# Self-attention: amplitude chain and logits ahead of two heads' sums, router's product two slots sooner, four heads' scores at once in the short tiles

## The chip, the cores and the metric

One core of a Trainium2 chip. The time is that of one execution on the device, in microseconds (us). The core has five engines with a queue each: PE (TensorE: matrix products and transposes), DVE (VectorE), ACT (ScalarE), POOL (GpSimd) and SP (SyncE, which here only issues DMAs). Every queue runs in its own order, and the queues meet at semaphores.

## The reference, cut to what matters

```python
x = x + cross_attention(layernorm(x), ctx)       # 2 x 512 rows, 2 x 8192 keys, 16 heads of 32
x = x + self_attention(layernorm(x))             # 2 x 512 rows, causal, 16 heads of 32
x = x + experts(layernorm(x))                    # 16 experts, top 2, capacity

# self attention, for a row x of 512:
q_amp, k_amp = softplus(x @ Wq_amp.T), softplus(x @ Wk_amp.T)       # split into 16 heads
q_phi, k_phi = pi * tanh(x @ Wq_phi.T), pi * tanh(x @ Wk_phi.T)
q_amp, k_amp = each / sqrt(mean(each ** 2 over the head) + eps)
scores = (q_amp cos q_phi . k_amp cos k_phi + q_amp sin q_phi . k_amp sin k_phi) / sqrt(32) * exp(scale)
out    = softmax(causal(scores)) @ (x @ Wv.T);  x = x + out @ Wo.T

# experts: logits = layernorm(x) @ w_router, softmax, top 2, rows of each expert counted in order
```

## The kernel before

The first 1550 us or so are the cross-attention. The change lies in the stage behind it, the self-attention, which runs from about 1550 us to about 1840 us of the profile; the experts follow to the end.

The 1024 rows are 8 row tiles t of 128 (four for each of two batches). Tile t attends to the tiles of its batch up to itself, so it has 1, 2, 3 or 4 blocks of 128 keys: `qb = t % 4`, `nk = 128 * qb + 128`. The 16 heads are taken in 8 pairs, so there are 64 steps p, with tile `a = p // 8` and pair `p % 8`. Two steps make a group of four heads, n = p // 2.

`self_order` writes out one list of pieces by hand, and each engine walks the list and emits its own part of each piece. Hence the place of a piece in the list is its place in the queue of the engine that does it. I call the 8 steps of a tile a block, numbered 0 to 7. A block has 16 slots k, two for each step, emitted by `slot(a, k)`. While block a attends, `ahead(a + 1, k)` prepares tile t = a + 1, and `follow` finishes tiles a - 1 and a - 2.

What `ahead` emits for tile t in block t - 1:
- slots 0 to 3: `p23` (PE, the product for the phases in four parts, banks 2 and 3), and on ACT `abs`, `exp`, `ln` (softplus of the amplitudes in banks 0 and 1, L1617 to L1625), `relu` (L1612) in slot 1, which frees banks 0 and 1
- slot 3 `amp` (DVE L1941: softplus finished), slot 4 `square` (DVE L1955) and `turn` (PE L1274: transposes the next tile), slot 5 `phase` and `mean` (DVE L1959, L1962)
- `phase` is a chain on ACT: a table load (L1509), Tanh (L1640), Sin (L1644), a wait for `tabs` (DVE L1973, the absolute value of the phase), Sin with a bias for the cosine (L1647), and a table load back (L1509)
- slot 6 `tabs`, and `p4` (PE, the product for the values, in two parts, bank 1); slot 7 the second part of `p4`, `copy` (ACT) and `low` (DVE L1951) of the next tile, and `mroot` (ACT L1514, L1516: the reciprocal root of the mean)
- slot 8 `vcopy` (ACT) and `norm` (DVE L1758 to L1968: a Newton step on the root, then the amplitudes are scaled); slots 9 and 10 `polar` 0 and 1 (DVE L1979: amplitude times cosine and sine); from slot 10 `qkT` (PE L1302: transposes of queries and keys), `qkC` (their copies), and the next tile's `p01` (PE)

What a step p does besides: `scoreT` (PE L1332: scores of a pair into banks 4 and 5; it waits until the step before has been read), `expT` (ACT L1671: exp of the pair into `pT`), and for each group n `cut` (DVE L2021, L2027: the causal mask on the last block of keys, then the blocks are added), `valueT` (PE L1347, L1351: the heads' sums over the keys; it waits for `cut`), and `normT` (DVE L2033, L2037: divides; it waits for `valueT`). `valueT` of group 4a stands behind slot 5 of block a.

Behind tile a - 1 follow `wo0` and `wo1` (PE L1362, slots 6 and 7), `x3` and the statistics; behind tile a - 2 come `router` (PE L1417, slot 4, bank 1) and `logit` (DVE L2058, L2061, slot 5), which frees bank 1 for `p4`. In block 1 a `colsum` (PE L1411) and `negsum` (DVE L2065) stand in their place, in block 6 also `cum` (PE L1425) and `place` (DVE L2114).

The queue of block a = 2 on PE, between its second and its sixth group of scores, is therefore: scoreT 17, p23, p23, scoreT 18, turn, router, valueT 8, scoreT 19, p4, wo0, p4, wo1, scoreT 20, valueT 9, scoreT 21, qkT.

A second list (`kept`) serves another numerical path, which is not taken with these inputs; `slot` and `ahead` are shared with it.

## Time and profile before

| | us |
|---|---|
| median of 3 runs | 1967.76 (1967.36 to 1967.77) |
| the profiled execution | 1968.28 |
| its span | 1966.5 |
| span busy: PE / DVE / ACT | 1898.0 / 1712.3 / 1470.9 |

The profile is one execution, recorded by the hardware. The rows further down come from four of its views: busy time in given stretches, with the clock that TensorE was granted (1.00 is full speed); the list of who waited for whom; the instructions in order of time; and instructions grouped by line. A name such as L1332 is a line of the kernel. An engine's row in the order of time ends with its idle time and the instruction that ended it, where there was any.

### The profile page before, as it was taken

To read this page: it belongs to the slowest core of one execution; us is meant where nothing else is said; L and a number is where in the kernel's file an instruction comes from. 1 tells how busy PE (TensorE), PEld (TensorE's weight loads), DVE (VectorE), ACT (ScalarE), POOL (GpSimd) and SP (SyncE) were. 2 spreads that over 40 slices of the span, in tenths; PEclk is the share of its full clock that TensorE was granted. 3 is DMA by queue.
4 is the path that set the end of the run, shared out by engine and by line. 5 is a ranking of instruction groups with operands and counts; after the bars stand their busy time and mean duration, and the time that the engine had idled before them with its cause. 6 is when DMAs were issued, how large, how long until landed. Compare 5 with 4: busy or idle time off the path is not lost.

```text
span 1966.5 us, 31028 instructions
## 1 busy us (share of the span) xinstructions
PE 1898.0 (97%) x11704; PEld 744.4 (38%) x11704; DVE 1712.3 (87%) x1530; ACT 1470.9 (75%) x1676; POOL 46.9 (2%) x57
## 2 busy tenths in 40 slices
PE   8999999999999999999999999999998989999895
PEld 4333333333333333333333333333332345556431
DVE  5799999999999999979999999999997578788655
ACT  2588888888888888778888888888887455555221
POOL 2000000000000000000000000000000000001103
PEclk9999999999999999999999999999999989999998
DMA  8333333333333333322332233333323000004785
GB/s 256 114 89 106 96 91 97 97 102 97 102 90 88 91 97 97 108 65 74 95 90 81 81 87 89 93 88 90 91 71 113 23 1 1 1 1 176 256 303 166
DMA packets 113674, 194.57 MB, mean 99 GB/s; under 512 B 10353, under 2 KB 64625, under 8 KB 113521
## 3 DMA queue, kind: packets, MB, share of 16 engines
q1 hardware_dynamic: 110528, 183.33, 31.8%
q0 software_dynamic: 2560, 8.39, 1.3%
q8 instruction: 98, 1.61, 0.3%
q10 hardware_dynamic: 432, 0.79, 0.1%
q14 instruction: 56, 0.45, 0.1%
HBM read 109.63 MB, written 50.33 MB: 81 GB/s over the span
## 4 chain that ended last, share of the span: by engine, by line
PE 87%; DVE 6%; issue 2%; ACT 2%; DMA 1%; POOL 1%; POOLq 0%; SPq 0%; DVEq 0%; ACTq 0%
PE ps L1204 24%; PE ps L1449 23%; PE ps L1103 12%; PE ps L1100 12%; PE ps L1293 2%; PE ps L1231 2%; PE ps L1288 2%; PE ps L1140 2%; PE ps L1256 1%; PE ps L1188 1%; PE ps L1332 1%; PE ps L1302 1%; DVE dacc L1860 1%; PE ps L1362 1%; ACT pt L1712 1%
## 5 line engine op out<-in xcount | busy, mean ns | idle before, releaser
L1712 ACT ACTIVATE pt<-ps,bias 128x1024 f32<-128x1024 f32 x1024 | 1108.7, 1114 | 212.3 <-PE ps L1449 211.3
L1860 DVE TENSOR_TENSOR dacc<-dacc,pt 128x2048 f32<-128x2048 f32 x496 | 1134.9, 2288 | 59.6 <-ACT pt L1712 35.9
L1449 PE MATMUL ps<-qst,kst 128*128 128x512 f16 x2048 | 611.1, 381 | 7.9 <-ACT pt L1712 7.9
L1204 PE MATMUL ps<-pt,vt 128*32 128x512 f32 x4096 | 493.4, 598 | 0.0
L1449 PEld LDWEIGHTS ps<-qst,kst 128*128 128x128 f16 x2048 | 178.1, 98 | 413.7 <-ACT pt L1712 123.3
L1103 PE MATMUL ps<-wsm 128*128 128x512 f16 x1152 | 310.8, 380 | 0.0
L1100 PE MATMUL ps<-wsm 128*128 128x512 f16 x1116 | 301.4, 379 | 0.0
L1204 PEld LDWEIGHTS ps<-pt,vt 128*32 128x32 f32 x4096 | 106.7, 109 | 262.6 <-issue 240.6
L1103 PEld LDWEIGHTS ps<-wsm 128*128 128x128 f16 x1152 | 112.8, 98 | 138.1 <-issue 3.3
L1100 PEld LDWEIGHTS ps<-wsm 128*128 128x128 f16 x1116 | 109.0, 98 | 133.1 <-issue 2.2
L1803 DVE SCALAR_TENSOR_TENSOR wsm<-ps,wsm 128x512 f16<-128x512 f32 x126 | 86.4, 686 | 26.2 <-ACT wsm L1533 26.2
L1671 ACT ACTIVATE pT<-ps 128x256 f32<-128x256 f32 (+3 forms) x64 | 44.5, 701 | 55.5 <-PE ps L1332 55.2
L1871 DVE TENSOR_TENSOR oacc<-ps,oacc 128x512 f32<-128x512 f32 x120 | 82.1, 684 | 2.3 <-PE ps L1209 2.3
L1537 ACT ACTIVATE vt<-ps 128x512 f32<-128x512 f32 x128 | 76.3, 596 | 3.8 <-PE ps L1103 3.8
L1533 ACT ACTIVATE wsm<-ps 128x512 f16<-128x512 f32 x126 | 74.4, 591 | 0.0
L2182 DVE SCALAR_TENSOR_TENSOR wsm<-wsm 128x512 f16<-128x512 f32 x90 | 61.5, 683 | 0.0
L1050 POOL DMA_INDIRECT xbuf<-xn,diu x13 | 14.3, 1097 | 1782.8 <-DVE diu L2131 1779.5
L1720 ACT ACTIVATE wsm<-wsm 128x512 f16<-128x512 f32 x90 | 55.8, 620 | 0.0
L1332 PE MATMUL ps<-QT,KT 64*128 64x128 f32 x640 | 53.1, 295 | 2.6 <-ACT pT L1671 2.2
L1293 PE MATMUL ps<-wsm,xT 128*128 128x512 f16 x216 | 50.8, 380 | 4.8 <-DVE negs L2065 2.3
L1332 PEld LDWEIGHTS ps<-QT,KT 64*128 64x128 f32 x640 | 41.5, 190 | 23.7 <-issue 23.7
L2033 DVE RECIPROCAL pr<-ps 128x128 f32<-128x128 f32 x32 | 30.5, 952 | 19.2 <-PE ps L1351 16.2
(228 smaller groups left out, 1201.2 us busy)
## 6 DMA issues: line engine op xcount, KB each, us to landing
kst<-kscr SPq DMA_DIRECT2D x132, 256.0 KB, 3.4
kscr<-wsm SPq DMA_DIRECT2D x126, 256.0 KB, 3.5
kst<-kst SPq DMA_DIRECT2D x124, 256.0 KB, 3.4
wsm<-in_ctx SPq DMA_DIRECT2D x31, 768.0 KB, 5.1
wx<-in_gate SPq DMA_DIRECT2D x10, 512.0 KB, 8.8
wx<-in_fc SPq DMA_DIRECT2D x10, 512.0 KB, 9.4
wx<-in_proj SPq DMA_DIRECT2D x10, 512.0 KB, 9.2
qst<-qscr SPq DMA_DIRECT2D x32, 128.0 KB, 3.0
```

The costliest lines, as they stand in the source:

```text
L1100: p = e.matmul(ps[:, at, :], wk[:, wi, c, u * 128:u * 128 + 128], chl[:, j, ci_, c, :], start=n == 0, stop=n == 8)
L1103: p = e.matmul(ps[:, at, :], chl[:, j, ci_, c, u * 128 - 512:u * 128 - 384], wv[:, wi, c, :], start=n == 0, stop=n == 8)
L1204: p = e.matmul(ps[32 * h:32 * h + 32, 4 + n % 2, :], vt[:, kb % 2, ch, c:c + 32], pt[:, (2 * i + h // 2) % 6, h % 2, :], start=ch == 0, st ...
L1293: p = e.matmul(ps[:, b0 + n, :], xhl[:, t % 2, xi, c * 128:c * 128 + 128], whl[w0 + n][:, wi, c, :], start=m == 0, stop=m == 11)
L1332: m = e.matmul(ps[:, bk + h, 128 * k:128 * k + 128], KT[64 * h:64 * h + 64, hp, c:c + 128], QT[64 * h:64 * h + 64, t % 3, hp, :], start=Tr ...
L1449: p = e.matmul(ps[:, 2 * half + h2, :], kst[:, kb % 2, h, ch * 128:ch * 128 + 128], qst[:, h, :], start=True, stop=True)
L1533: e.activation(halves(kb, u)[:, 0], ps[:, at, :], ACT.Copy, scale=KS / (WS * CS)).then_inc(S["khi"], 1)
L1537: e.activation(vt[:, j, u - 4, :], ps[:, at, :], ACT.Copy, scale=1.0 / (WS * CS)).then_inc(S["vev"], 1)
L1712: e.activation(pt[:, (2 * i + half) % 6], ps[:, 2 * half:2 * half + 2, :], ACT.Exp, bias=bias[:, 4 * kb + ch:4 * kb + ch + 1], scale=SCORE ...
L1803: e.scalar_tensor_tensor(out=hl[:, 1], in0=ps[:, at, :], scalar=KS / (WS * CS), in1=hl[:, 0], op0=ALU.mult, op1=ALU.subtract).then_inc(S[" ...
L1860: e.tensor_tensor(own_heads, own_heads, probs, ALU.add).then_inc(S["add"], 1)
L1871: e.tensor_tensor(oacc[:, g, :], ps[:, 4 + n % 2, :], oacc[:, g, :], ALU.add).then_inc(S["oac"], 1)
```

## The change

In `ahead` the amplitude pieces go up: `amp`, `square` and `mean` follow `ln` in slot 2, `mroot` stands ahead of `phase` in slot 5, and `norm` behind `tabs` in slot 6. On DVE they thereby stand ahead of `normT` of group 4a - 1 and `cut` of group 4a, and on ACT the root is taken ahead of the phase's table load. In `slot` the router's product and `colsum` go from slot 4 to slot 2 ahead of `p23`, and `logit` and `negsum` from slot 5 to slot 2, behind `mean`. `valueT` of group 4a goes from behind slot 5 to behind slot 6, hence behind the first part of `p4` and `wo0`. Block 7 keeps its order. `pairs_of(p)` is 2 for even and 0 for odd steps in tiles with one or two blocks of keys (blocks 0, 1, 4, 5): there `scoreT` and `expT` take two pairs at once, the second pair in the upper half of the same two banks, so that 16 of the 64 `scoreT` and `expT` fall away.

```diff
--- before.py
+++ after.py
@@ -459,32 +459,32 @@
             out.append((("abs", "exp", "ln")[slot], t))
         if slot == (1 if t else 3) and t < 7:
             out.append(("xn", t + 1))
-        if slot == 3:
+        if slot == (2 if t else 3):
             out.append(("amp", t))
             if t < HALVES:
                 empty((0, 1), "amp", t + 1)
-        elif slot == 4:
             out.append(("square", t))
+            out.append(("mean", t))
+        if slot == 4:
             if t < 7:
                 turn(t + 1)
         elif slot == 5:
+            out.append(("mroot", t))
             out.append(("phase", t))
             empty((2, 3), "phi", t + 1)
-            out.append(("mean", t))
         elif slot == 6:
             out.append(("tabs", t))
+            out.append(("norm", t))
             p4(t, 0)
         elif slot == 7:
             if t < 7:
                 out.append(("copy", t + 1))
                 if t + 1 >= HALVES:
                     out.append(("low", t + 1))
-            out.append(("mroot", t))
             p4(t, 1)
             empty((1,), "sv", t + 1)
         elif slot == 8:
             out.append(("vcopy", t))
-            out.append(("norm", t))
         elif slot == 9:
             out.append(("polar", t, 0))
         elif slot == 10:
@@ -536,29 +536,33 @@
 
     def slot(a, k):
 
+        if a == 6 and k == 2:
+            out.append(("cum", 0, 1, fill((1,))))
+        if a == 1 and k == 2:
+            out.append(("colsum", 0, fill((1,))))
+            empty((1,), "lg", 1)
+        if 2 <= a < 7 and k == 2:
+            follow(a - 2, "router")
         if a < 7:
             ahead(a + 1, k)
+        if a == 1 and k == 2:
+            out.append(("negsum", 0))
+        if 2 <= a < 7 and k == 2:
+            follow(a - 2, "logit")
+        if a == 6 and k == 2:
+            out.append(("place", 0, 1))
+            empty((1,), "cumr", 1)
         if 1 <= a < 8:
             for step in (carry if a < 7 else late).get(k, ()):
                 follow(a - 1, step)
-        if a == 6 and k == 4:
-            out.append(("cum", 0, 1, fill((1,))))
-        if a == 1 and k == 4:
-            out.append(("colsum", 0, fill((1,))))
-            empty((1,), "lg", 1)
-        if a == 1 and k == 5:
-            out.append(("negsum", 0))
         if (a, k) in halving:
             out.append(halving[a, k])
-        if 2 <= a < 8 and k == (4 if a < 7 else 1):
+        if a == 7 and k == 1:
             follow(a - 2, "router")
-        if 2 <= a < 8 and k == (5 if a < 7 else 2):
+        if a == 7 and k == 2:
             follow(a - 2, "logit")
         if a == 5 and k in (6, 8, 9, 11, 13):
             out.append((("rank", "odds", "first", "second", "shares")[(6, 8, 9, 11, 13).index(k)], 0))
-        if a == 6 and k == 5:
-            out.append(("place", 0, 1))
-            empty((1,), "cumr", 1)
         if a == 6 and k == 7:
             out.append(("rows", 0))
 
@@ -623,11 +627,13 @@
     else:
         for p in range(64):
             a, k = p // 8, 2 * (p % 8)
-            if p <= 56:
+            if p <= 56 and pairs_of(p):
                 out.append(("scoreT", p, ()))
             if 56 <= p < 63:
                 out.append(("scoreT", p + 1, fill((0, 1)) if p == 56 else ()))
             slot(a, k)
+            if p % 8 == 3 and a < 7:
+                out.append(("valueT", p // 2 - 1))
             if p == 63:
                 out.append(("rank", 1))
                 out.append(("first", 1))
@@ -635,13 +641,14 @@
                 out.append(("moments", 4 + k // 4))
             if p == 8:
                 out.append(("stats", 1))
-            out.append(("expT", p))
+            if pairs_of(p):
+                out.append(("expT", p))
             if p % 2:
                 if p > 2:
                     out.append(("normT", p // 2 - 1))
                 out.append(("cut", p // 2))
             slot(a, k + 1)
-            if p % 2 == 0 and p:
+            if p % 2 == 0 and p and (p % 8 != 2 or a == 7):
                 out.append(("valueT", p // 2 - 1))
         ahead_of_last()
         out.append(("woT", 7, 0, 3, (("prob", 63),)))
@@ -675,6 +682,11 @@
 
 def score_bank(p):
     return 0 if p >= 56 and p % 2 else 4
+
+
+def pairs_of(p):
+
+    return (2 if p % 2 == 0 else 0) if p // 8 % 4 < 2 else 1
 
 
 def turn_bank(j):
@@ -1326,12 +1338,13 @@
                     e.wait_ge(S["KT"], 2 * t + hp // 4 + 1)
                     if x is not None:
                         e.wait_ge(S["prob"], x + 1)
-                    for k in range(qb + 1):
-                        for h in range(2):
-                            c = 128 * ((4 * b + k) % 5)
-                            m = e.matmul(ps[:, bk + h, 128 * k:128 * k + 128], KT[64 * h:64 * h + 64, hp, c:c + 128],
-                                         QT[64 * h:64 * h + 64, t % 3, hp, :], start=True, stop=True)
-                    m.then_inc(S["score"], 1)
+                    for j in range(pairs_of(p)):
+                        for k in range(qb + 1):
+                            for h in range(2):
+                                c, o = 128 * ((4 * b + k) % 5), 256 * j + 128 * k
+                                m = e.matmul(ps[:, bk + h, o:o + 128], KT[64 * h:64 * h + 64, hp + j, c:c + 128],
+                                             QT[64 * h:64 * h + 64, t % 3, hp + j, :], start=True, stop=True)
+                    m.then_inc(S["score"], pairs_of(p))
                 elif what == "valueT":
                     n, t, g, u = t, t // 4, t % 4, t % 2
                     qb, b = t % 4, t // 4
@@ -1665,11 +1678,16 @@
                                      scale=-1.0, accum_out=rsum[:, s:s + 1]).then_inc(S["prob"], 1)
                 elif what == "expT":
                     p, n, bk, nk = t, t // 2, score_bank(t), 128 * (t // 8 % 4) + 128
-                    e.wait_ge(S["score"], p + 1)
+                    e.wait_ge(S["score"], p + pairs_of(p))
                     if n > 1:
                         e.wait_ge(S["value"], n - 1)
-                    e.activation(pT[:, n % 2, 2 * (p % 2):2 * (p % 2) + 2, 0:nk], ps[:, bk:bk + 2, 0:nk], ACT.Exp,
-                                 scale=-1.0).then_inc(S["prob"], 1)
+                    if pairs_of(p) == 2:
+                        e.activation(pT[:, n % 2, :, 0:nk].rearrange("p (j h) n -> p j h n", j=2),
+                                     ps[:, bk:bk + 2, :].rearrange("p h (j n) -> p j h n", j=2)[:, :, :, 0:nk], ACT.Exp,
+                                     scale=-1.0).then_inc(S["prob"], 2)
+                    else:
+                        e.activation(pT[:, n % 2, 2 * (p % 2):2 * (p % 2) + 2, 0:nk], ps[:, bk:bk + 2, 0:nk], ACT.Exp,
+                                     scale=-1.0).then_inc(S["prob"], 1)
                 elif what == "pT" and t % 2:
                     n, nk = t // 4, 128 * (t // 16 % 4) + 128
                     e.wait_ge(S["pT"], t + 1)
```

## Rows read from the trace of the kernel before

**Rows 1.** Stretches, blocks 0 to 6: length, busy PE, PEld, DVE, ACT, POOL; PEclk; DMA.

```profile
1578.09:1610.80 32.71, 27.39 (x149) 13.97 (x148) 23.73 (x37) 18.86 (x28) 0.00 (x0) 0.84 0.00 1
1610.80:1643.69 32.89, 30.62 (x253) 17.54 (x252) 29.49 (x54) 18.48 (x29) 0.00 (x0) 0.95 0.00 1
1643.69:1677.45 33.76, 31.63 (x318) 19.69 (x317) 26.42 (x48) 19.39 (x26) 0.00 (x0) 1.00 0.01 1
1677.45:1716.10 38.65, 35.97 (x381) 23.06 (x380) 29.25 (x52) 21.11 (x26) 0.00 (x0) 0.96 0.01 1
...
1745.43:1777.20 31.77, 29.25 (x254) 16.96 (x253) 25.05 (x55) 17.73 (x27) 0.00 (x0) 1.00 0.00 1
1777.20:1810.19 32.99, 28.82 (x326) 19.08 (x325) 27.62 (x54) 19.06 (x26) 9.38 (x8) 0.95 0.45 159
```

**Rows 2.** Who waited for whom, PE, 1578 to 1810 us: sum, times, longest.

```profile
PE ps L1302 <- DVE qc L1979: 11.9, 6, 3.3
PE ps L1293 <- DVE negs L2065: 2.3, 1, 2.3
PE ps L1293 <- DVE lg L2061: 2.1, 4, 0.7
```

**Rows 3.** In order of time, PE, block 2: start, duration, instructions, idle before.

```profile
1651.62 0.94 PE L1332 MATMUL ps<-QT,KT 64*128 64x128 f32 x12
1652.48 0.66 PE L1274 MATMUL ps<-ident,xn 128*128 128x128 f32 x4
1652.98 0.96 PE L1417 MATMUL ps<-wr,aR 128*128 128x16 f32 x8
1653.87 0.86 PE L1347 MATMUL ps<-pT,sv 128*32 128x128 f32 x24
...
1656.29 1.47 PE L1293 MATMUL ps<-wsm,xT 128*128 128x512 f16 x6 [0.47 <-DVE lg L2061]
...
1662.41 0.94 PE L1332 MATMUL ps<-QT,KT 64*128 64x128 f32 x12
...
1666.96 0.63 PE L1302 MATMUL ps<-ident,qc 128*128 128x128 f32 x4 [1.67 <-DVE qc L1979]
```

**Rows 4.** In order of time, ACT, block 2.

```profile
1647.90 1.06 ACT L1625 ACTIVATE t<-t 128x1024 f32<-128x1024 f32 x1
...
1652.60 0.81 ACT L1671 ACTIVATE pT<-ps 128x768 f32<-128x768 f32 x1 [2.75 <-PE ps L1332]
1653.43 1.28 ACT L1509 ACT_TABLE_LOAD   x1
...
1661.04 0.23 ACT L1514 ACTIVATE mr<-ms 128x32 f32<-128x32 f32 x1
```

**Rows 5.** In order of time, DVE, block 2.

```profile
1651.81 1.22 DVE L1941 TENSOR_TENSOR amp<-amp,t 128x1024 f32<-128x1024 f32 x1
...
1656.15 1.22 DVE L1973 SCALAR_TENSOR_TENSOR t<-phi 128x1024 f32<-128x1024 f32 x1
1657.28 0.95 DVE L2033 RECIPROCAL pr<-ps 128x128 f32<-128x128 f32 x1
...
1660.70 0.69 DVE L2021 TENSOR_TENSOR pT<-pT,trib 128x512 f32<-128x512 f32 x1 [2.15 <-ACT pT L1671]
...
1663.24 0.18 DVE L1758 TENSOR_TENSOR mt<-mr 128x32 f32<-128x32 f32 x1
...
1665.59 2.36 DVE L1979 TENSOR_TENSOR qc<-qc,amp 128x1024 f32<-128x1024 f32 x2
```

**Rows 6.** In order of time, PE, block 5.

```profile
1752.80 0.71 PE L1332 MATMUL ps<-QT,KT 64*128 64x128 f32 x8
...
1766.66 0.63 PE L1302 MATMUL ps<-ident,qc 128*128 128x128 f32 x4 [1.51 <-DVE qc L1979]
```

**Rows 7.** Groups by line and shape, ACT, 1578 to 1830 us: busy, mean ns.

```profile
L1671 ACT ACTIVATE pT<-ps 128x512 f32<-128x512 f32 x16 | 9.5, 592 | 12.7 <-PE ps L1332 12.6
...
L1671 ACT ACTIVATE pT<-ps 128x256 f32<-128x256 f32 x16 | 6.1, 382 | 15.8 <-PE ps L1332 15.7
```

## The prediction

> **What bounds the kernel now.** I read the busy time block by block first [rows 1]. A block of the self-attention lasts 29 to 39 us, and PE is busy for all of it but 2 to 5 us; DVE is busy for 24 to 29 us. So PE sets the time, but only just: whoever takes PE's idle time away meets DVE soon after. The clock column says that three of the later blocks also ran partly at half speed. Block 1 has 0.95 over 32.89 us. With levels of 1.0 and 0.5 that is 0.05 x 32.89 / 0.5 = 3.3 us at the lower one (1.2 GHz), in which a busy PE loses 1.6 us. Block 3 loses 1.5 us and block 6 up to 1.6 us in the same way. Block 0 (0.84) spends 10.5 us there.
>
> Then the list of waits [rows 2]: of PE's idle time, 11.9 us in six pieces is `qkT` waiting for `polar` (qc), and 2.3 + 2.1 = 4.4 us is `p4` waiting for `negsum` or `logit` to free bank 1. The moved pieces bear on these two. The six pieces lie in blocks 0 and 2 to 6 and last 3.3, 1.7, 1.8, 1.4, 1.5 and 2.2 us; those of blocks 2 and 5 stand as rows [rows 3, 6].
>
> The order of time in block 2 shows the chain behind the large wait [rows 3 to 5]. The third scores (scoreT 18) start at 1651.62, their exp at 1652.60, the table load at 1653.43; the phase ends, and exp 19 lets `cut` start on DVE at 1660.70. Behind `cut` and `low` come the root's Newton steps at 1663.24, `polar` at 1665.59, and `qkT` at 1666.96. So the amplitudes are normalized last, although nothing but the order of the queues demands it.
>
> **Part by part: the logits.** The router's product takes 1653.87 - 1652.98 = 0.9 us of PE [rows 3] and moves ahead of the third and fourth `p23`. It costs PE nothing but puts these, scoreT 18 and all of ACT's phase back by 0.9 us. On DVE the amplitude chain and the logits took 1651.81 to 1656.15 = 4.3 us [rows 5]. They now begin when `ln` ends (1647.90 + 1.06 = 1648.96 in block 2 [rows 4]) and end at 1653.4, while `p4` is not reached before 1655.3. The 4.4 us of waits go. In block 5 some 0.1 us is left, since `ln` comes later there; in block 1 `colsum` must first wait about 0.6 us for `relu`, and `p4` about 1 us for `negsum`, instead of 2.3.
>
> **The sums of group 4a.** `normT` of 4a - 1 and `cut` of 4a now lie behind these 4.3 us on DVE. In block 2 `cut` 8 ends at 1653.4 + 1.25 + 2.0 = 1656.6 instead of just ahead of 1651.81. `valueT` 8 would have waited for it; at its new place, behind `p4` and `wo0`, it comes up at 1658.3, so it waits for nothing. But it had covered something: scoreT 19 has to wait until exp 18 has read the banks. Between them lay turn, router and `valueT` (1652.48 to 1653.87 and 1.0 us more), of which only the turn (1652.98 - 1652.48 = 0.5 us) stays. exp 18 starts 0.98 us after scoreT 18, takes 0.81 us [rows 3, 4], and some 0.15 us later PE may go on: 1.95 us after the start of scoreT 18, against 0.86 + 0.5 = 1.4 us of work. New wait in blocks 2 and 6: 0.55 and 1.05 us (no turn in block 6); in block 3, with larger scores and an exp of 1.0 us, 0.8 us. Blocks 0, 1, 4 and 5 no longer have this step.
>
> **What happens to `qkT`.** Its new time is the start S of the third scores plus a chain L. For block 2, S = 1651.62 + 0.9 = 1652.5. L is: start of scores to start of exp 0.98, exp 0.81, `mroot` 2 x 0.23 and gaps 0.5, table load 1.28, Tanh 1.1, `tabs` 1.25, `norm` (1663.24 to 1665.59) 2.35, `normT` 0.95 + 0.3, `cut` and `low` (1660.70 to 1663.24) 2.55, `polar` 2.36 / 2 = 1.2, handing over 0.3 [rows 3 to 5]. Together 13.6 us, so `qkT` starts at 1666.1 instead of 1666.96: 0.9 us gained, not the 2.1 us that PE idled. DVE works from 1648.96 to 1666 almost without a pause, so **DVE becomes the bound in the first half of a block**. PE itself reaches scoreT 20 at 1662.45 (1662.41 before) and then waits 0.6 us for `cut` 9.
>
> The other blocks repeat the pattern (seven of it; blocks 2 and 5 stand as rows). In block 5, S = 1752.80 + 0.9 - 0.2 = 1753.5 and L = 13.6 (exp of 1.0 us, two instead of three pieces of `cut`, 0.45 us for `rank`), so `qkT` starts at 1767.1, against 1766.66 [rows 6]: 0.5 us lost. ACT's root and the later scores put the phase back, and the exp that used to gate `cut` 21 was no long wait. By the same sum, with each block's own exp and `cut`: block 0 +0.85, block 1 +0.9, block 2 +0.9, block 3 +1.35, block 4 +0.25, block 5 -0.5, block 6 +0.1 (`rows` still lies ahead of `polar` 7). **Sum 3.85 us.** After `qkT` the second half of each block keeps its length, PE and DVE both having the same work from there.
>
> **Four heads at once.** On PE, 12 instructions of scores last 0.94 us and 8 last 0.71 [rows 3, 6], so one more costs 0.055 to 0.06; from start to next start 12 take 1652.48 - 1651.62 = 0.86, so a group has a fixed share of about 0.2 us. 16 groups fewer make 3.2 us of PE time, but those in front of `qkT` only lengthen the wait there. The last group of blocks 0, 1, 4 and 5 lies behind `qkT`: 4 x 0.2 = **0.8 us**. On ACT a pair of 256 elements takes 0.382 us and one of 512 takes 0.592 [rows 7], so one of 512 in place of two of 256 saves 0.17 us, off the path. No row has the four-head pattern of two strided pieces. Bounds: what one instruction of that size takes now, and twice the old pair; I take the first, since the 0.81 us of 768 elements [rows 4] lies on one line with these two: 0.17 us and 0.82 ns an element, whatever banks are read. By it 1024 elements take 1.0 us.
>
> The Trainium skill (TensorEngine Tiling, Key Properties) says that a change of tiling mode, not merely of the tile, drains the engine. `scoreT` uses row tiles and `valueT` column tiles; standing next to each other they made three changes, apart they make four. By that rule and the 0.2 us fixed share as an estimate, blocks 1 to 6 pay up to 1.2 us; I find no such price on its own in the rows, and my sum leaves it out.
>
> **The clock.** Block 3's half-speed stretch followed `qkT`'s 1.8 us of idle time, block 6's its 2.2 us and 1.0 us more, block 1's its 2.3 us in front of `p4`. In block 3 the single gap falls apart into pieces of 0.8 and 0.7 us far from each other, in block 6 into 1.05, 0.7 and 0.7. I expect full speed there: +1.3 us (block 3) and +0.7 us (block 6, where DVE bounds part of it), **2.0 us**. Block 1's is contained in its 0.9. In block 5 PE now idles 1.5 us and, after 0.8 us of work, 1.25 us more. That is more than block 3's 1.8 us, so I expect a new stretch: **-1.6 us**. Block 4 (0.9 and 1.35 us) stands between block 2, which kept its clock after 0.47 and 1.67 us, and block 3; I count it as kept. Block 0 keeps its stretch.
>
> **The sum.** 3.85 + 0.8 + 2.0 - 1.6 = 5.05 us. The profiled execution takes 1968.28 us (span 1966.5 and 1.8 around it) and would take 1963.2; it stands 0.5 us over the median, so the median goes from 1967.76 to **1962.7**. The experts behind the stage shift with it. No moved piece issues a DMA. The first expert weights are issued on SP behind `p4` of tile 7 and the scatters on POOL behind `rows`, which come some 1.5 us later relative to `qkT`'s block; PE does not need either for 40 us.
>
> **Rivals.**
> (B) Full speed throughout blocks 1 to 6. For it: no single wait is left above 1.5 us. Against: block 5's two gaps lie close together. 5.05 + 1.6 = 6.65 us: 1961.1.
> (C) The waits only change their name. Blocks 1, 4 and 5 (or 5 and two others) fall to half speed, since DVE's chain leaves PE two gaps in each. 6.65 - 3 x 1.6 = 1.85 us: 1965.9. For it: DVE's 25 to 29 us per block [rows 1], and that I may have missed 0.3 us a block in chains of a dozen hand-overs, which gives the same time. Against: PE does reach `p4` earlier in all blocks. That the change does little of what it says, because ACT's phase starts 0.9 to 1.5 us later than before, is this case too.
> (D) Slower. One mechanism: in each of blocks 1 to 6 the two gaps in front of `qkT` bring a half-speed stretch as long as block 0's (10.5 us, with some 5.2 us of PE's work in it, 2.6 us lost). 6 x 2.6 - 6.65 = +8.95: 1976.7. It decides from a loss of 1.1 us per block, and is measurably slower from 1.75. Against: block 0 idles over 5 us, the others 1.5 to 2.8.
>
> **Chances.** My forecast 0.40, B 0.20, C 0.32, D 0.08. A measurement of this kernel can tell about 0.2%, 3.9 us, from no change, so the border is 1963.8. Of my forecast's 0.40 I put 0.04 beyond the border (its terms are good to about 1 us). Faster 0.36 + 0.20 = 0.56; same 0.04 + 0.32 = 0.36; slower 0.08. The range of 8 in 10 goes from 1959.5 (B, with 0.2 us more a block) to 1968.0 (C with all its mishaps).
>
> **What would show it.** `p4`'s waits for lg and negs should be gone but for about 1 us in block 1. `qkT`'s waits for qc, 11.9 us, should be about half, and new ones appear: `valueT` on `cut`'s output (3 to 5 us in all), scores on exp about 2.4 us in blocks 2, 3 and 6. The clock should be 1.00 in blocks 3 and 6, below it in block 5. DVE should have hardly a pause between `ln` and `polar`. I am wrong if `qkT` starts over 2 us sooner after the third scores than L says, if `cut` 8 is late for `valueT` 8, or if the clock falls in more than two of blocks 1 to 6.

## The result and the profile after

The changed kernel takes 1956.55 us (median of 4 runs, 1955.53 to 1958.81) against 1967.76 us for the kernel before: a ratio of 0.9943, 95% interval 0.9926 to 0.9960, or 11.2 us less. The prediction was 1962.7 us with a range from 1959.5 to 1968.0 us. So the sign was right and the size too small. Two more comparisons on other chips, made for the experiments below, gave 0.9959 (0.9946 to 0.9973) and 0.9964 (0.9951 to 0.9976): 8.0 and 6.4 us less. Times are medians of all executions of a kernel; the ratios leave out three slow executions of two variants, of 3263, 7862 and 8430 us.

The profiled execution of the changed kernel takes 1958.81 us (span 1957.0), that of before 1968.28 us (span 1966.5): 9.5 us apart.

The stretches by block of the changed kernel, with the columns of [rows 1]:

```profile
1577.09:1607.33 30.24, 25.04 (x149) 12.90 (x148) 23.21 (x37) 19.03 (x24) 0.00 (x0) 0.89 0.00 1
1607.33:1639.12 31.79, 28.65 (x253) 16.48 (x252) 29.43 (x53) 17.33 (x24) 0.00 (x0) 1.00 0.00 1
1639.12:1671.88 32.76, 32.06 (x318) 19.54 (x317) 26.98 (x49) 19.30 (x26) 0.00 (x0) 1.00 0.00 1
1671.88:1707.42 35.54, 34.72 (x381) 22.14 (x380) 29.15 (x52) 21.01 (x26) 0.00 (x0) 1.00 0.01 2
1707.42:1736.08 28.66, 26.85 (x222) 14.69 (x221) 23.68 (x44) 15.42 (x22) 0.00 (x0) 1.00 0.01 1
1736.08:1767.78 31.70, 28.80 (x254) 16.42 (x253) 25.18 (x56) 17.30 (x23) 0.00 (x0) 1.00 0.00 1
1767.78:1800.55 32.77, 28.59 (x326) 18.34 (x325) 28.09 (x56) 18.90 (x25) 7.78 (x8) 0.97 0.39 137
```

Blocks 0 and 3 lost most, 2.5 and 3.1 us; block 5 is as long as before. The clock column is the second thing to see: 1.00 in blocks 1 to 5, block 5 among them, where the prediction had a new half-speed stretch, and 0.97 in block 6, where it had full speed.

The list of PE's waits from 1570 to 1800 us (sum, times, longest), which answers [rows 2]:

```profile
PE ps L1375 <- ACT phi L1653: 4.8, 5, 1.5
PE ps L1360 <- DVE pT L2039: 3.5, 1, 3.5
PE ps L1345 <- ACT pT L1689: 3.2, 4, 1.2
PE ps L1314 <- DVE qc L1997: 2.8, 4, 1.7
PE ps L1314 <- DVE xs L2064: 1.5, 2, 1.0
PE ps L1424 <- ACT amp L1625: 0.9, 1, 0.9
PE ps L1305 <- DVE negs L2083: 0.8, 1, 0.8
PE ps L1360 <- DVE pr L2045: 0.6, 1, 0.6
PE ps L1305 <- DVE lg L2079: 0.3, 1, 0.3
```

`p4`'s 4.4 us are down to 0.8 + 0.3. `qkT`'s 11.9 us are down to 2.8. At the top stands a wait that the prediction doesn't have: 4.8 us in which the first half of `woT` (L1375) waits for the Tanh to free bank 3. Block 5 in order of time on PE (answers [rows 6]) shows where it lies:

```profile
1744.03 1.16 PE L1345 MATMUL ps<-QT,KT 64*128 64x128 f32 x16
...
1746.07 1.47 PE L1305 MATMUL ps<-wsm,xT 128*128 128x512 f16 x6 [0.29 <-DVE lg L2079]
1749.08 1.98 PE L1375 MATMUL ps<-wo,aT 128*128 128x512 f32 x4 [1.54 <-ACT phi L1653]
1750.99 0.64 PE L1360 MATMUL ps<-pT,sv 128*32 128x128 f32 x16
...
1757.44 0.63 PE L1314 MATMUL ps<-ident,qc 128*128 128x128 f32 x4 [0.58 <-DVE qc L1997]
```

From the third scores (1744.03) to `qkT` (1757.44) it is 13.4 us; the prediction's L was 13.6. What PE used to idle in one piece in front of `qkT` it now idles in two, first for the Tanh and then for `polar`.

A better yardstick than blocks are the stretches between the first `qkT` of one tile and that of the next, numbered 0 to 6: stretch n ends at the `qkT` of tile n + 1, which lies in block n (busy PE, PEld, DVE, ACT, POOL, then PEclk and DMA). Of before, those that end at the `qkT` of tiles 2, 5 and 7:

```profile
1599.50:1633.84 34.34, 32.07 (x232) 17.61 (x233) 28.81 (x46) 21.86 (x30) 0.00 (x0) 0.87 0.00 1
...
1703.27:1736.27 33.00, 30.93 (x269) 17.98 (x269) 26.18 (x47) 17.26 (x26) 0.00 (x0) 0.95 0.01 2
...
1766.66:1801.22 34.56, 31.68 (x332) 19.46 (x333) 28.80 (x64) 18.48 (x25) 2.29 (x3) 1.00 0.16 53
```

and of the changed kernel:

```profile
1597.23:1629.50 32.27, 29.13 (x233) 16.06 (x233) 28.78 (x46) 21.89 (x27) 0.00 (x0) 0.95 0.00 1
...
1696.24:1727.12 30.88, 29.07 (x271) 16.81 (x269) 25.51 (x47) 17.79 (x24) 0.00 (x0) 1.00 0.01 2
...
1757.44:1791.11 33.67, 31.76 (x333) 19.19 (x333) 28.63 (x64) 17.64 (x24) 0.47 (x1) 1.00 0.09 31
```

All seven add up to 235.28 us before and 226.17 us after: 9.1 of the 9.5 us lie here. In front of the first `qkT` 1.0 us was gained and behind the last one 0.6 us lost. In the two later traces of the changed kernel the seven take 227.31 and 227.58 us.

### The profile page after: what moved, and what is told of

It is laid out like the page before. It is cut to its first block, busy times and chain, and to the rows that moved or that the text cites. A ratio compares the mean times of both kernels' runs of the same rounds, so it can differ in the third digit from the quotient of the medians.

```text
span 1957.0 us, 30984 instructions
## 1 busy us (share of the span) xinstructions
PE 1892.4 (97%) x11704; PEld 741.0 (38%) x11704; DVE 1712.8 (88%) x1530; ACT 1469.1 (75%) x1660; POOL 45.2 (2%) x57
## 4 chain that ended last, share of the span: by engine, by line
PE 88%; DVE 5%; ACT 2%; issue 2%; DMA 1%; POOL 1%; POOLq 0%; SPq 0%; DVEq 0%; ACTq 0%
PE ps L1216 24%; PE ps L1462 23%; PE ps L1115 12%; PE ps L1112 12%; PE ps L1305 3%; PE ps L1243 2%; PE ps L1345 2%; PE ps L1268 1%; PE ps L1152 1%; PE ps L1200 1%; PE ps L1300 1%; PE ps L1314 1%; DVE dacc L1878 1%; PE ps L1360 1%; ACT pt L1730 1%
## 5 line engine op out<-in xcount | busy, mean ns | idle before, releaser
L1689 ACT ACTIVATE pT<-ps 128x768 f32<-128x768 f32 (+1 forms) x32 | 28.9, 916 | 31.2 <-PE ps L1345 31.0
L1345 PE MATMUL ps<-QT,KT 64*128 64x128 f32 x640 | 48.9, 291 | 3.2 <-ACT pT L1689 3.2
L1243 PE MATMUL ps<-wx,xeT 128*64 128x512 f32 x160 | 43.3, 593 | 0.7 <-ACT xeT L1584 0.7
```

Of the source, the lines that this page charges most:

```text
L1243: p = e.matmul(ps[64 * c:64 * c + 64, 6 + s, :].rearrange("p (w n) -> p w n", w=2), xeT[:, s, k * 128 + 64 * c:k * 128 + 64 * c + 64], wei ...
L1345: m = e.matmul(ps[:, bk + h, o:o + 128], KT[64 * h:64 * h + 64, hp + j, c:c + 128], QT[64 * h:64 * h + 64, t % 3, hp + j, :], start=True, ...
```

## Experiments

Two theories run through all of them. The first: my sum of shorter waits was about right, and the rest is TensorE's clock. The second: the waits themselves shrank by far more than the sum said. Beside each time stands the sum of the seven stretches from `qkT` to `qkT` ("the seven"). The first four variants had no run of the changed kernel beside them on their chip; they are compared with it by their ratios to the kernel before and by the seven.

### Each part taken back alone

One pair of heads per group of scores:

```diff
 def pairs_of(p):
-    return (2 if p % 2 == 0 else 0) if p // 8 % 4 < 2 else 1
+    return 1
```

> The changed kernel with one pair of heads per group of scores everywhere (16 more groups and 16 more exponentials). Theory 1 (my sum: only the four groups behind the last transposes of q and k count, 0.2 us each): 0.8 us slower than the changed kernel, about 1957.4 us. Theory 2 (the groups in front of them count too, because the second scores of a pair must wait 0.55 to 0.8 us until the exponential has read the banks, now that the sums no longer stand between them): 0.8 + 4 x 0.65 = 3.4 us slower, about 1960.0 us, with new waits of scores on pT in blocks 0, 1, 4 and 5.

Measured: 1957.93 us beside 1966.02, ratio 0.9959 (0.9947 to 0.9971), the seven 225.4 us. That is no slower than the changed kernel, as far as an interval of over 2 us to either side can tell. Of Theory 2's new waits for pT there are 2.0 us in block 0 and 0.2 us each in blocks 1 and 5, and nothing came of them, since they stand ahead of `qkT`, which is bound elsewhere. The stretches say more than the time. Those to tiles 3 and 7 are 0.23 and 0.19 us longer than in the changed kernel: the 0.2 us of the last group, as predicted. But the one to tile 6 is 0.41 us shorter. ACT in block 5 of this kernel, and of the changed one:

```profile
1747.54 0.60 ACT L1689 ACTIVATE pT<-ps 128x512 f32<-128x512 f32 x1 [3.49 <-PE ps L1345]
```

```profile
1745.29 1.02 ACT L1685 ACTIVATE pT<-ps 128x1024 f32<-128x1024 f32 x1 [3.74 <-PE ps L1345]
```

The exp follows the start of its scores by 0.76 us and takes 0.60 here, with four heads at once 1.26 and 1.02, and the table load and the Tanh wait for it. So the merged group costs 0.9 us in the chain to `qkT`, of which its earlier start gives back 0.5. **Merging the scores gains behind `qkT` and loses about as much in front of it.**

The logits at their old slots (router at slot 4, logit at slot 5, with colsum, negsum, cum and place):

```diff
-        if 2 <= a < 7 and k == 2:
-            follow(a - 2, "router")
...
+        if 2 <= a < 8 and k == (4 if a < 7 else 1):
+            follow(a - 2, "router")
+        if 2 <= a < 8 and k == (5 if a < 7 else 2):
+            follow(a - 2, "logit")
```

> The changed kernel with the router's product and the logits (and their kin) back at the slots they had before. Theory 1 (DVE's queue ahead of the polar form bounds the first half of a block, so the order of its pieces matters little): p4's waits for negs and lg come back, but qkT starts within 0.3 us of where it does now; 0 to 1.5 us slower than the changed kernel, 1956.5 to 1958.0 us. Theory 2 (the logits at their old place stand between the tabs and norm, and everything behind them is late by their 1.6 us in five blocks, less the 0.9 us by which the third scores start sooner): 3.5 us slower, about 1960 us.

Measured: 1963.85 us, ratio 0.9992 (0.9982 to 1.0001), the seven 232.1 us. Theory 1 is out; Theory 2 forecast a loss, but too small a one and in the wrong place. The list of PE's waits:

```profile
PE ps L1301 <- DVE lg L2075: 8.2, 4, 2.9
PE ps L1301 <- DVE negs L2079: 4.3, 1, 4.3
```

These are 12.5 us where the kernel before had 4.4 [rows 2]. DVE in block 2 shows why:

```profile
1651.25 0.95 DVE L2047 RECIPROCAL pr<-ps 128x128 f32<-128x128 f32 x1
...
1654.69 0.23 DVE L2075 SCALAR_TENSOR_TENSOR lg<-ps,rs,shift 128x16 f32<-128x16 f32 x1
1654.84 1.22 DVE L1987 SCALAR_TENSOR_TENSOR t<-phi 128x1024 f32<-128x1024 f32 x1
```

With the other parts in place the logits (L2075) stand behind the whole amplitude chain and behind `normT` and `cut` of group 4a (from L2047 on, 3.1 us), and the tabs (L1987) come right after them. `p4`, which comes up at 1653.2, waits for all of that, and everything behind it is late. Theory 2 had the logits between the tabs and `norm`.

The normalizing at its old place:

```diff
         elif slot == 5:
-            out.append(("mroot", t))
             out.append(("phase", t))
...
         elif slot == 6:
             out.append(("tabs", t))
-            out.append(("norm", t))
...
+            out.append(("mroot", t))
             p4(t, 1)
...
             out.append(("vcopy", t))
+            out.append(("norm", t))
```

> The changed kernel with the root of the mean square and the normalizing of the amplitudes back behind the fourth pair's cut, their place before; the square and mean stay early. Theory 1 (DVE works without a pause between ln and polar): the same 2.35 us are only shifted, 0 to 1 us slower in all, 1956.5 to 1957.5 us. Theory 2 (norm at its new place fills DVE's idle time while ACT makes phases and exponentials): DVE would have idled about 1 us a block there; seven blocks give 5 to 7 us, 1961.5 to 1963.5 us. A stretch at half speed that comes or goes would add or take 1.5 us each.

Measured: 1969.33 us, ratio 1.0016 (1.0005 to 1.0027), slower than the kernel before; the seven 239.7 us. Theory 2, and twice its price. DVE in block 3 of this kernel (idle before, and what ended it):

```profile
1688.57 1.23 DVE L1991 SCALAR_TENSOR_TENSOR t<-phi 128x1024 f32<-128x1024 f32 x1 [0.31 <-ACT phi L1653]
1691.92 0.96 DVE L2051 RECIPROCAL pr<-ps 128x128 f32<-128x128 f32 x1 [2.13 <-PE ps L1364]
...
1697.71 1.23 DVE L1986 TENSOR_TENSOR amp<-amp,mr 128x1024 f32<-128x1024 f32 x1
1698.97 2.36 DVE L1997 TENSOR_TENSOR qc<-qc,amp 128x1024 f32<-128x1024 f32 x2
```

and in block 3 of the changed kernel:

```profile
1686.34 1.23 DVE L1991 SCALAR_TENSOR_TENSOR t<-phi 128x1024 f32<-128x1024 f32 x1 [0.69 <-ACT phi L1653]
...
1688.58 1.23 DVE L1986 TENSOR_TENSOR amp<-amp,mr 128x1024 f32<-128x1024 f32 x1
1689.84 0.96 DVE L2051 RECIPROCAL pr<-ps 128x128 f32<-128x128 f32 x1
```

After the tabs DVE waits 2.13 us for the sums of `valueT`, which now come behind `woT`. In the changed kernel `norm` fills just this gap: the `normT` behind it (L2051) finds its sums there. In front of `polar` `norm` costs its whole 2.35 us; here it costs almost nothing.

The sums of the first two heads' pairs at their old place:

```diff
-            if p % 8 == 3 and a < 7:
-                out.append(("valueT", p // 2 - 1))
...
-            if p % 2 == 0 and p and (p % 8 != 2 or a == 7):
+            if p % 2 == 0 and p:
                 out.append(("valueT", p // 2 - 1))
```

> The changed kernel with the sums of the first two heads' pairs back at their old place, behind the fourth p23 and in front of p4. Theory 1 (cut of the pair ends 1 to 2 us after PE gets there): PE waits for pT in blocks 1 to 6 by about 1 us each, partly in place of the wait in front of qkT and of the scores' 0.8 us wait: 1 to 3 us slower, 1957.5 to 1959.5 us. Theory 2 (that wait would only replace others): no difference within 0.5 us.

Measured: 1965.11 us, ratio 0.9999 (0.9989 to 1.0009), the seven 237.3 us. Theory 1's mechanism at more than twice its price:

```profile
PE ps L1358 <- DVE pr L2043: 13.6, 5, 3.3
PE ps L1358 <- DVE pT L2037: 5.3, 2, 3.5
```

`cut` now lies behind the amplitude chain and the logits, and PE waits up to 3.3 us for it with `p4` and `woT` queued behind.

### One part alone

The amplitude chain alone in the kernel before (mean, mroot and norm move as in the change, nothing else does):

```diff
-        if slot == 3:
+        if slot == (2 if t else 3):
             out.append(("amp", t))
...
         elif slot == 5:
+            out.append(("mroot", t))
             out.append(("phase", t))
...
             out.append(("tabs", t))
+            out.append(("norm", t))
```

> The kernel before with the amplitude chain alone moved (amp, square and mean behind ln, the root in front of the phase, norm behind the tabs); logits, sums and scores as they were. Theory 1 (norm ahead of cut is what makes qkT early, as the 12 us that its return costs suggest): 5 to 8 us faster than before, 1958 to 1961 us. Theory 2 (with the logits still in the middle of the phase and the first sums in front of p4, the parts need one another; alone it moves the wait to valueT and p4): 0 to 2 us faster, 1964 to 1966 us.

Measured: 1968.80 us beside 1965.94, ratio 1.0013 (1.0000 to 1.0025), the seven 240.3 us: not faster, rather slower. Theory 2's idea was right and its number too good. The first line of its waits names the reason:

```profile
PE ps L1347 <- DVE pr L2027: 11.9, 5, 3.6
```

L2027 is the second half of `cut`, which now stands behind the amplitude chain, while the sums that wait for it still stand in front of `p4`. So what the three moves are worth can't be split. Taken back singly they cost about 6, 11 and 7 us, together some 24, where all of them bring 8. The logits alone or the sums alone were not run.

### The clock

Again the changed kernel, beside more runs of before:

> The changed kernel itself, beside the kernel before in more runs than the first comparison had. The runs of before lie on a line: 1.56 us more for each 0.001 by which the mean granted clock is lower. Theory 1 (the granted clock of the changed kernel is higher by 0.003 to 0.004, worth about 5 us, and the rest, about 4 to 5 us, is PE's shorter wait at the same clock): runs of the changed kernel between 1954 and 1961, median 1956.5 to 1957.5 us, and about 1960.5 us at clock 0.990 where before has 1964.8. Theory 2 (the clock is noise of the first comparison, and all of the 11.2 us is shorter waits): the same clock in both kernels, and the distance of 11 us in every pair of runs.

Measured: 1957.99 us beside 1965.94, ratio 0.9959 (0.9946 to 0.9973). Neither theory in full: the clock was higher by 0.003 on the mean (0.992 against 0.989), as Theory 1 says, but the distance was 8 us, not the 9 to 10 of Theory 1 or the 11 of Theory 2. Within the 22 runs of the kernel before beside it the time follows the clock: 1.4 us more for each 0.001 less, with a correlation of 0.95.

First I filled PE's idle time with products nobody reads, in both kernels:

```diff
+                elif what == "spin":
+                    for name, value in ev[-1]:
+                        e.wait_ge(S[name], value)
+                    for k in range(ev[3]):
+                        e.matmul(ps[:, ev[2], :], xT2[:, 1, 0:128], xT2[:, 1, :], start=True, stop=True)
```

> The changed kernel with nine matrix products whose result nobody reads in PE's two idle times of block 0 (six of 0.46 us in the 3.5 us in front of the second sums, three in the 1.7 us in front of the first transposes of q). Theory 1 (the half-speed stretch of block 0 comes from these idle times): block 0 at clock 1.00, and the 2.5 us that its work lost come back, less up to 0.4 us by which the fillings are late: about 1954.5 us. Theory 2 (the stretch has another cause, such as the low activity of the whole block): no gain, or a loss of up to 0.5 us, about 1956.8 us.

> The kernel before with 24 products whose result nobody reads in PE's idle times of block 0 and in front of the first transposes of q of blocks 2 to 6. The order of all work stays as it is. Theory 1 (the clock follows from the length of these idle times, and it makes more of the gain than my sum had): mean clock up by 0.003 to 0.004, half-speed stretches of blocks 0, 3 and 6 gone, 4 to 6 us faster than before, about 1961 us. Theory 2 (all but about 2 us of the gain is shorter waits): within 2 us of before, about 1965 us.

Measured: 1959.33 us (0.9964, 0.9951 to 0.9976) and 1969.34 us (1.0014, 1.0005 to 1.0023). Both runs say little: one such product over 512 columns of f32 is two instructions of 0.46 us, so six filled 5.4 us where 3.5 were idle. The clock did rise (to 0.994 and 0.993), and the overfilling ate it. With 256 columns each, and sized to the gaps (below, the places in the kernel before; in the changed kernel seven in front of the second sums and three in front of `qkT`, in block 0 alone; the later version of the kernel before has five instead of six in block 0):

```diff
+            if t:
+                out.append(("spin", t, 2, (6, 0, 3, 3, 2, 2, 4)[t - 1], fill((2,))))
             qkT(t, 0, 0)
...
+                        if t == 1:
+                            e.matmul(ps[:, ev[2], 0:256], xT2[:, 1, 0:128], xT2[:, 1, 0:256], start=True, stop=True)
+                        else:
+                            e.matmul(ps[:, ev[2], 0:256], ident[:], wo2[:, k % 4, 0:256], start=True, stop=True)
```

> The kernel before with 20 products of 0.46 us whose result nobody reads, now sized to stay inside PE's idle times: six in the 3.3 us in front of qkT of block 0, three, three, two, two and four in those of blocks 2 to 6 (the earlier filling had taken 10 us more than the gaps held, since a product of that type over 512 columns is two instructions). Theory 1 (idle time alone brings the half-speed stretches, and these make up most of what my sum missed): clock up from 0.989 to 0.993, 4 to 6 us faster than before, about 1961 us. Theory 2 (the clock is a by-product; the gain was shorter waits): 1965 to 1966 us. Theory 3 (fillings at the ends of chains cost more than they look, since they put qkT off by up to half a filling each): 1966 to 1968 us at a clock of 0.993.

> The changed kernel with ten such products in block 0: seven (3.2 us) in the 3.5 us in front of the second sums, three (1.4 us) in the 1.7 us in front of qkT. Theory 1: block 0 at full speed, which gives back 1.6 to 2.3 us: about 1955 us at a clock of 0.994 or 0.995. Theory 2 (no gain from the clock): 1957 to 1958 us.

Measured: 1970.93 and 1969.66 us beside 1970.70 (0.9994, 0.9980 to 1.0008, and 0.9991, 0.9977 to 1.0005). The seven took 231.5 and 224.6 us, so the stage had gained; the time was lost behind it, in stalls that are the subject of the last section. So the question was put again on another chip:

> The changed kernel itself, as the base on this chip. From qkT of tile 0 to qkT of tile 7 it took 226.2 and 227.3 us in its two traces, the kernel before 235.3 us. Theory 1 (the stalls on the instruction side belong to one chip or to the fillings, not to the change): 1956 to 1959 us where the kernel before takes 1966 to 1968 us. Theory 2 (they come on any chip by the run and hit the changed kernel more): within 3 us of the kernel before on this chip.

> The changed kernel with ten fillings in block 0, again. Its stretch from qkT to qkT was 224.6 us. Theory 1 (the clock of block 0 is worth what the stretch shows): 1.6 to 2.7 us faster than the changed kernel on the same chip, at a clock higher by 0.001 to 0.002. Theory 2 (what block 0 gains, a later gap loses): no difference.

> The kernel before with 19 fillings (one fewer in block 0, where they had put qkT off). Its stretch from qkT to qkT was 231.5 us against 235.3. Theory 1 (idle time alone brings the half-speed stretches): 3 to 5 us faster than the kernel before, at a clock higher by 0.003. Theory 2 (the stretch gains, the time does not): within 1 us.

Measured, beside 1965.48 us of the kernel before: the changed kernel 1959.10 us (0.9964, 0.9951 to 0.9976), with its block 0 filled 1956.55 us (0.9950, 0.9937 to 0.9964), the kernel before with its gaps filled 1962.87 us (0.9985, 0.9976 to 0.9994). Without any change in the order of work **the filling makes either kernel 2.6 us faster** (for the kernel before the interval leaves no doubt; for the changed one the two intervals overlap, but the slowest of its five filled runs, 1957.23 us, is faster than the fastest of the six unfilled ones beside it, 1958.22 us). The seven go from 235.3 to 231.1 us in the one and from 227.6 to 224.6 us in the other. Two stretches of the kernel before with its gaps filled, ending at the `qkT` of tiles 2 and 5:

```profile
1596.78:1628.60 31.82, 29.49 (x233) 16.52 (x233) 28.69 (x46) 21.76 (x30) 0.00 (x0) 0.95 0.00 1
...
1698.02:1729.33 31.31, 30.30 (x273) 17.91 (x273) 26.00 (x47) 17.27 (x26) 0.00 (x0) 1.00 0.00 1
```

They lasted 34.34 and 33.00 us at clocks of 0.87 and 0.95. In the kernel before the clock stands at half from 1703.7 to 1707.1 us, right behind the 1.8 us of idle time in block 3; in both filled traces it stays full there and the stretch takes 31.31 us. Nothing but idle time in front of `qkT` was taken away, so that idle time is shown to be the cause of the half-speed stretch, and the stretch cost 1.7 us. The other gaps gave little: behind those of blocks 2, 4 and 5 (1.7, 1.4 and 1.5 us) the clock had been 1.00 anyway and the stretches are the same to 0.01 us; behind block 6 (2.2 us) the clock rose from 0.89 to 1.00 over 15 us, but the rest of the kernel took 165.1 us instead of 165.3. And the stretch to tile 2 in the changed kernel with block 0 filled:

```profile
1595.12:1625.81 30.69, 27.55 (x233) 15.32 (x233) 28.77 (x46) 21.79 (x27) 0.00 (x0) 1.00 0.00 1
```

It was 32.27, 33.44 and 33.67 us in the three traces without filling. Between the two filled kernels the seven differ by 1.26, 1.13, 1.26, 1.42, 0.44, 0.08 and 0.89 us, in all **6.5 us: this is the gain without the clock**, but for the stretch to tile 2, where the filled kernel before still had 0.95. In its earlier trace, with one filling more in block 0, that stretch was at 1.00 and took 31.62 us, by which the 6.5 would be 6.3. `p4`'s wait was filled in neither, so it does not decide about the clock there.

### The wait that was missed, and a better version

`woT`'s first half behind the second `p4`, where the Tanh is over:

```diff
-    carry = {6: ["wo0"], 7: ["wo1"], 10: ["x3"], 11: ["stat"], 12: ["lroot"], 13: ["lnr", "xn3"], 14: ["rT"], 15: ["rC"]}
+    carry = {7: ["wo0", "wo1"], 10: ["x3"], 11: ["stat"], 12: ["lroot"], 13: ["lnr", "xn3"], 14: ["rT"], 15: ["rC"]}
```

> The changed kernel with the first half of the output projection behind the second p4 instead of ahead of the first two heads' sums, so that the Tanh, which frees its bank, is over when PE comes to it. Theory 1 (the 4.8 us of PE's waits for phi are real losses, since qkT waits only 3.2 us in all): they go, 1 to 1.5 us come back as waits of the sums for cut in blocks 1 and 5, and DVE's chain lets half of the rest through: 1.5 us faster than the changed kernel. Theory 2 (DVE's chain from tabs to polar sets qkT in all blocks, and the wait moves in front of qkT): the same time, within 0.5 us.

and with the cut of the second two pairs in DVE's idle time before the tabs in blocks 0 and 4 (and `valueT` waiting for `aT` there, since `cut` no longer orders them):

```diff
+            if p % 8 == 3 and a % 4 == 0:
+                out.append(("cut", p // 2))
             slot(a, k)
...
-                out.append(("cut", p // 2))
+                if p % 8 != 3 or a % 4:
+                    out.append(("cut", p // 2))
```

> As the kernel with the output projection behind, and in blocks 0 and 4 the cut of the second two pairs ahead of the tabs, in DVE's idle time before the Tanh (2.9 us in block 0, 1.1 us in block 4). Theory 1 (DVE's chain from the Tanh to polar sets qkT there): it gets 0.68 us shorter in each, and the second sums of block 0 need not wait for cut behind norm; 1.4 us faster than the kernel with the projection behind, 3 us faster than the changed kernel. Theory 2 (PE sets qkT): no difference between these two.

Both ran beside the stalls (1968.28 and 1969.35 us beside 1970.70: 0.9980, 0.9968 to 0.9992, and 0.9976, 0.9963 to 0.9989); what can be read is the seven. With `woT` behind, the 4.8 us of waiting for phi are gone, and the stretches are 32.30, 32.03, 31.62, 34.88, 30.87, 30.31, 33.68 us. Five of the seven are those of the changed kernel to 0.01 us; the one to tile 3 is 0.24 us shorter, and the one to tile 2 varies anyway. So PE's missed wait cost 0.24 us in block 2, where PE reaches `qkT` without a wait, and nothing elsewhere: there the chain of ACT and DVE sets `qkT`, and Theory 2 holds. With `cut` moved as well, the stretches of blocks 0 and 4 are 31.63 and 30.27 us, 0.67 and 0.60 us shorter: the 0.68 us of one `cut`, as Theory 1 says for DVE's chain. All of it with nine fillings in block 0:

> The changed kernel with the output projection behind the second p4, cut ahead of the tabs in blocks 0 and 4, and nine fillings in block 0. The stretch from qkT to qkT was 225.0 us without the fillings. Theory 1 (the gains add up): 223.3 us for the stretch, 3 us faster than the changed kernel, about 1954 us. Theory 2 (DVE's chain lets only the fillings through): as the changed kernel with fillings alone.

Measured, beside 1965.48 us: 1955.62 us (0.9949, 0.9936 to 0.9963), the seven 223.1 us, the shortest of all. The gains add up in the stretches. In the time this version beats both kernels, but it can't be told from the changed kernel with block 0 filled.

## Why the prediction fell short

The prediction's sum, put on the seven stretches (`qkT`'s gain of a block, the 0.2 us of a merged group where one ends in the stretch, and the clock's terms where they lie), against the three traces of the changed kernel (gains over the trace of the kernel before; the last column is the gain between the two filled kernels, where nearly all is at full speed):

| stretch | predicted | measured | both kernels filled |
|---|---|---|---|
| 0 | 0.85 | 1.3, 1.3, 1.3 | 1.3 |
| 1 | 0.9 + 0.2 | 2.1, 0.9, 0.7 | 1.1 |
| 2 | 0.9 + 0.2 | 1.3, 1.3, 1.3 | 1.3 |
| 3 | 1.35 | 1.4, 1.4, 1.4 | 1.4 |
| 4 | 0.25 + 1.3 (clock) | 2.1, 2.1, 2.1 | 0.4 |
| 5 | 0.2 - 0.5 | 0.1, 0.1, 0.1 | 0.1 |
| 6 | 0.1 + 0.2 - 1.6 (clock) | 0.9, 0.9, 0.9 | 0.9 |
| behind | 0.7 (clock) | -0.6, 0.6, 0.1 | |
| sum | 5.05 | 8.5, 8.6, 7.8 | 6.5 |

**The logits and `p4`.** Right: 1.1 us of its waits left, as forecast, 0.8 us of it in block 1.

**The sums of 4a.** Half right. The scores wait for exp 3.2 us in four pieces (forecast 2.4 in three, measured 2.0 there; the fourth, 1.2 us, lies behind block 6's `qkT`). `valueT` waits 3.5 + 0.6 us for `cut`, as forecast in sum, but the 3.5 lie in block 0 and the 0.6 behind block 6's `qkT`. Ahead of `qkT` in blocks 1 to 6 PE comes too late to wait, since it waited for the Tanh before; with `woT` behind, these waits are back (0.2 to 1.0 us). That `woT` would meet the Tanh was overlooked, though the prediction's terms hold it: in block 2 they put the end of the Tanh at 1652.5 + 4.7 = 1657.2, and `wo0` behind a `p4` of 1.3 us at 1656.6. By the run with `woT` behind it cost 0.24 us.

**`qkT` as S + L.** The mechanism was right, and without the clock (last column) the stretches 0 to 4 came within 0.45 us each. The term that was mis-sized is L: with the clock left out, the seven gave 6.5 us where the sum had 4.65. The chain of a dozen steps was taken a little long, 13.6 us against 13.4 in blocks 2 and 5, the two for which the prediction gives it; S came within about 0.1 us in both. The largest miss of this kind was block 6, 0.9 instead of 0.3 us, for which the prediction shows no chain; which step was too long there stays open. That DVE works almost without a pause between `ln` and `polar` holds but for its wait for the Tanh, 0.3 to 1.2 us in blocks 1 to 6 and 2.9 us in block 0. Ahead of amp it keeps 18 us of idle time in six blocks. What the change does is fill the holes of DVE's chain *behind* the tabs.

**The clock.** Of the 2.8 to 3.6 us by which the three traces passed the sum, L is 1.8 and the clock the other 0.9 to 1.7, and here lies the largest single term. Block 3's stretch went, as forecast, and gave 1.7 us instead of 1.3. The new one of block 5 (-1.6 us) came in none of the three traces. The step that failed reads "PE now idles 1.5 us and, after 0.8 us of work, 1.25 us more". In fact it idles 1.5 us for the Tanh, works for 7.8 us (1749.08 to 1756.86), and idles 0.6 us: the missed wait took over the idle time and moved it to a place of its own. That is not all, as the run with `woT` behind shows, where PE does not wait for the Tanh:

```profile
1755.30 0.65 PE L1360 MATMUL ps<-pT,sv 128*32 128x128 f32 x16 [0.23 <-DVE pr L2045]
...
1757.12 0.63 PE L1314 MATMUL ps<-ident,qc 128*128 128x128 f32 x4 [0.96 <-DVE qc L1997]
```

Here the two gaps stand where the prediction had them, but they are 0.23 and 0.96 us long instead of 1.5 and 1.25, and the clock is 1.00 behind them too. So the lengths of the gaps were wrong, the first above all.

Block 0 kept its stretch in all three traces, as forecast, and filling it is worth 2.6 us. Behind block 6 the traces differ, with the same gaps of 1.0, 0.6 and 1.2 us (the changed kernel's first trace, then its second):

```profile
1791.11:1806.11 15.00, 12.23 (x164) 10.32 (x166) 12.27 (x25) 6.31 (x10) 7.72 (x8) 0.89 1.04 380
```

```profile
1789.26:1804.26 15.00, 11.82 (x181) 10.03 (x181) 13.22 (x27) 7.04 (x11) 7.73 (x8) 1.00 1.05 383
```

The third is like the second. From the last `qkT` to the end they took 165.9, 164.6 and 165.2 us, the kernel before 165.3: the 0.7 us did not come on the mean, and in the kernel before filling that gap gave 0.2 us. As a mechanism, rival B (full speed in blocks 1 to 6) is what happened in two of the three traces, and in blocks 1 to 5 of the first. Its gain of 6.65 us is 1.3 us short of the second comparison's 8.0, mostly by L's error, and 0.3 us above the third's 6.4.

**Four heads at once.** Forecast 0.8 us, measured nothing in the time. The 0.2 us of a group do show in the stretches to tiles 3 and 7. But the prediction priced the merging only by what it saves behind `qkT`. In front of it the longer scores and exp lengthen the chain by 0.9 us in block 5, and the stretch by 0.4.

**The change of tiling mode.** The prediction weighed a rule of the Trainium skill (TensorEngine Tiling (Array Packing), Key Properties), that a change of mode drains the engine, at up to 1.2 us lost. No run isolates it; the stretches came out shorter than the sum that left it out, so there is no sign of it here, though other terms could hide it.

**The first comparison.** 11.2 us against 8.0 and 6.4 in the later ones. Of the 32 runs of the kernel before beside the first experiments, the shortest took 1961.08 us at a mean clock of 0.992 and the longest 1970.49 us at 0.987. The first comparison had four runs of before, near the long end (1967.36 to 1969.52 us; the profiled one at 0.988), and four of the changed kernel at 0.991 to 0.994. On the later chips without stalls the kernel before took 1966.0, 1965.9 and 1965.5 us. So of the 6.2 us by which the first comparison passed the forecast, 2.6 to 4.8 us are the luck of few runs (11.2 less the 6.4 to 8.6 us that the later comparisons and the three traces show). The remaining 1.4 to 3.6 us are the two errors above. The ratios of both later comparisons lie inside the range, whose lower end is 1959.5 / 1967.76 = 0.9958, the second one, 0.9959, only just: the range left little room on the fast side, and the error of L has one sign in all stretches.

The rivals C (new half-speed stretches) and D (slower) had nothing to stand on: no trace of the changed kernel shows a half-speed stretch in blocks 2 to 5. None of the three signs of being wrong that the prediction names came either; they looked for large errors, and the two that there were are small.

## What to carry to other kernels

When several engines hand work round in a ring, a piece has no price of its own. Moved into a hole of its engine's queue `norm` cost nearly nothing, and at the end of the same queue 11 us in seven blocks; taken back singly, the logits, the sums and the normalizing each cost nearly all that the three bring or more, and the normalizing alone brought nothing. So list each engine's holes first, with what ends them, and ask of each moved piece which hole it fills and who then stands behind it. Idle time of TensorE is worth more than its length where it lowers the clock: filling gaps of 1.4 to 3.5 us with work that nobody reads gained 2.6 us here, nearly all of it behind two of them (3.3 and 1.8 us in the kernel before). Overfilling gives it back: 24 fillings twice as long made the kernel before 3.4 us slower. And compare kernels within a fraction of a per cent only over many runs, since one program's times spread by 9 us, in step with its mean clock.
